# Cross attention keys: three of four groups turned by DVE in 32 by 32 blocks and transfers through DRAM, in place of PE transposes

## The chip, the core and the metric

The kernel runs on one core of a Trainium2 chip. The metric is the device time of one execution in microseconds (us). The engines are PE (TensorE: matmuls and transposes through an identity), DVE (VectorE), ACT (ScalarE), POOL (GpSimd) and SP (SyncE, which here only waits and issues DMAs). They run their own instruction streams and meet only at semaphores.

## The reference, cut to what matters

A decoder layer on 16 batches of 100 tokens of width 512: self attention, cross attention over 361 context rows per batch, and a ternary feed-forward. The change is in the cross attention:

```python
q = x @ Wq.T                                   # 32 heads of 16
k = rmsnorm(heads(context @ Wk.T)); v = heads(context @ Wv.T)
scores = einsum('bhnd,bhmd->bhnm', rmsnorm(q), k) * 16 ** -0.5
out = einsum('bhnm,bhmd->bhnd', softmax(scores), v)
```

## The kernel before, in words

Self attention comes first (to about 545 us), cross attention second (to about 1033 us), the feed-forward last. Only the middle stage is touched.

The 16 x 361 context rows are cut into 46 chunks of 126 rows (`KC`), regardless of where a batch ends. Batch b projects two or three new chunks (two only for batches 7 and 14, which the code calls `short`); the chunk on a border is shared by two batches. A chunk's projected keys lie with the rows on the partitions and 512 columns (4 groups of 8 heads of 16). The scores need them the other way round: 128 columns of a group on the partitions. So for each of the four groups t, `turn_heads(b, t)` transposes the 126x128 blocks of the two or three chunks on PE into the PSUM tile `B[0]`, and `keys_back(b, t)` copies them on ACT into `kT` (a second copy puts the shared rows into the next batch's half of `kT`).

`turn(b)` is one round of the stage on each engine, with the order written by hand. On PE a turn runs the six score units `scores2(b, 1)` to `scores2(b, 5)` and then `scores2(b+1, 0)`; unit u covers two of the twelve (group, chunk) pairs, so unit 0 needs group 0 alone, and unit 1 is the first that needs group 1. Between them lie the projections of batch b+1 (`project2`, twelve matmuls each: 1 to 3 keys, 4 to 6 values), the products with the values (`attend2`), queries (`project_q`, `turn_queries`), and the transposes of finished outputs (`out_turn`). `turn_heads(b, 2)` and `turn_heads(b, 3)` stand in turn b, `turn_heads(b+1, 0)` and `turn_heads(b+1, 1)` in turn b. In three turns (2, 7 and 12) `project2(b+2, 1)` is pulled ahead into the end of the turn, where it waits for `ctx_lo` (DVE, L1221).

The keys of batch b+1 are made during turn b: ACT copies the projections into `raw` and squares them (`keep_raw`), DVE sums and takes the inverse root (`square_sums`, `rms_start`, `rms_step`, the last of them L1282), POOL multiplies (`normed`, L595: one instruction for queries when there are new ones, then one for each chunk). DVE then goes on to `x2_lo`, `add_cross(.., 0)` (which waits for PE's `out_turn(.., 0)`), `queries_back` (L1298) and `ctx_lo`. PE's `turn_heads(b+1, 0)` waits for `queries_back`, as both use `B[0]`.

SP issues, in each turn b, `sixteenth(2b, 0)`, `sixteenth(2b+1, 1)` (L520, parts of the feed-forward weights, first eight turns) and `context(b+2)` (L513), each behind waits.

Of the kernel before, what the change touches and what calls it, by code (L numbers as in the profile page):

```python
# [6 lines left out]
F32 = mybir.dt.float32  # L7
# [19 lines left out]
KC = 126  # L27
NC = 3
# [185 lines left out]
def build(nc, x, wqkv, wo, wx, ctxt, wffn, gains, bcols, consts, rope, out):  # L214
    with ExitStack() as ctx:
# [45 lines left out]
        raw = [carve([KC, 4, 512]) for _ in range(2)]  # L261
# [7 lines left out]
        carve([128, 12288 - 4096 - 2 * CTXP * KT - 2 * NT * CTXP - 3 * XH * VW])  # L269
# [3 lines left out]
        e = carve([KC, 6, HT * S])  # L273

# [99 lines left out]

        A = [ctx.enter_context(nc.psum_tensor(f"A{i}", [128, 512], F32)) for i in range(2)]
# [4 lines left out]
        def hidden_banks(u, e):  # L380
# [24 lines left out]
                   pe_xT2=1, pe_q=1, pe_qT=1, pe_proj=6, pe_T=4, pe_sc=6, pe_pv=4, pe_oT=2,  # L405
                   a_ctx=1, a_x2=1, a_sqq=1, a_sq2=3, a_v2=3, a_T=4, a_e=6, a_o=4, a_abs=3,
                   d_xn2=1, d_ctx=1, d_x2=1, d_ssqq=1, d_ssq2=3, d_rstd2=1, d_qT=1, d_on=2, d_x2out=2,
                   g_qn=1, g_kn=3, g_m=1,
# [26 lines left out]
        g_ones = sem("g_ones")  # L435
        d_warm, a_ws, g_wlo, a_z = sem("d_warm"), sem("a_ws"), sem("g_wlo"), sem("a_z")
# [28 lines left out]
        def _(sp):  # L465
# [59 lines left out]

            context(0)
            context(1)
            sp.wait_ge(*count("d_x1", TL - 1, 1))
            for b in range(NB - 2):
                if b < NB // 2:  # L530
                    sixteenth(2 * b, 0)
                    sixteenth(2 * b + 1, 1)
                context(b + 2)
                if b == NB // 2:
                    for n in range(2):
                        sp.wait_ge(*count("a_abs", NB - 2 + n, 3))
                        tile(n)
                elif b == NB // 2 + 3:
                    sp.wait_ge(d_tern, 2)
                    tile(2)  # L540

            for n in range(3, 12):
# [6 lines left out]
                tile(n)  # L549

# [8 lines left out]
        def _(pool):  # L559
# [95 lines left out]
            pool.memset(kT[:, :, :, 2 * KC:CTXP], 0.0)  # L655
# [32 lines left out]
        def _(act):  # L688
# [115 lines left out]
            def keep_raw(b, n, par):  # L804
# [4 lines left out]
                if n == 1:  # L809
                    act.wait_ge(*count("pe_T", b - 2, 4))  # L810
# [26 lines left out]
            def keys_back(b, t):  # L837

                act.wait_ge(*count("pe_T", b, t + 1))
# [3 lines left out]
                ins = act.activation(kT[:, b % 2, t, 0:whole], B[0][:, 0:whole], ACT.Copy)  # L843
                if b < NB - 1:
                    act.wait_ge(*count("pe_sc", b - 1, T_UNITS[t]))
                    ins = act.activation(kT[:, 1 - b % 2, t, 2 * KC + own:CTXP], B[0][:, tail + own:tail + KC], ACT.Copy)
                ins.then_inc(sig["a_T"], 1)

# [116 lines left out]
            keys_back(0, 0)  # L965
            keys_back(0, 1)
# [5 lines left out]
            def turn(b, par, end):  # L972
# [5 lines left out]
                keys_back(b, 2)  # L978
# [7 lines left out]
                keys_back(b, 3)  # L986
# [25 lines left out]
                if end < 2:  # L1012
                    if not short(b + 1):
                        values(b + 1, 2, odd)
                    keys_back(b + 1, 0)
# [8 lines left out]
                if end < 2:  # L1024
                    keys_back(b + 1, 1)
# [50 lines left out]
        def _(dve):  # L1076
# [211 lines left out]
            def queries_back(i):  # L1288
# [12 lines left out]
                ins.then_inc(sig["d_qT"], 1)  # L1301

# [284 lines left out]
            add_attn(TL - 1, A[0])  # L1587
            x2_lo(1, B[0])
            square_sums_q(1)

            def turn(b, par, end):
# [25 lines left out]
                else:  # L1617
# [6 lines left out]
                    ternary(4, 0)  # L1624
                if end == 1:
# [3 lines left out]
                if x2_tile(b) is not None:  # L1629
                    x2_lo(x2_tile(b), B[0])  # L1630
                if o2_tile(b) is not None:
                    add_cross(o2_tile(b), 0)
                if end == 1:
# [96 lines left out]
        def _(pe):  # L1730
# [143 lines left out]
            def turn_heads(b, t, par):  # L1874
# [4 lines left out]
                ins.then_inc(sig["pe_T"], 1)  # L1879

            def scores2(b, u):
                if u == 0:
                    pe.wait_ge(*count("a_T", b, 1))
                    pe.wait_ge(*count("d_qT", last_tile(b), 1))
                if u > 0:
# [3 lines left out]
                for f in range(2):  # L1889
                    t, c = divmod(2 * u + f, NC)  # L1890
                    for r in range(RT):
                        ins = pe.matmul(C[r][0:KC, f * 2 * S:(f + 1) * 2 * S],  # L1892
                                        kT[32 * r:32 * r + 32, b % 2, t, c * KC:(c + 1) * KC],
# [414 lines left out]
```

## Time and profile before

| what | value |
|---|---|
| three runs | 1312.74, 1312.95 and 1315.94 us, median 1312.95 |
| the profiled execution | 1312.68 us; its span, first to last instruction, 1310.9 us |
| PE busy | 1268.3 us, 97% of the span |
| DVE, ACT, POOL busy | 781.7, 648.9 and 295.8 us |
| PE transposes of the keys (L1878) | 184, 32.4 us busy |
| DMA engines' share over the span | 13.4% on the queue of the program's own transfers |

Sums are made against the profiled execution. An instruction's busy time overlaps its neighbours' on PE, so what a group costs is read from start to start in the timeline, not from its busy time.

### The profile page before, as it was taken

To read this page: it belongs to the slowest core of one execution; us is meant where nothing else is said; L and a number is where in the kernel's file an instruction comes from. 1 tells how busy PE (TensorE), PEld (TensorE's weight loads), DVE (VectorE), ACT (ScalarE), POOL (GpSimd) and SP (SyncE) were. 2 spreads that over 40 slices of the span, in tenths; PEclk is the share of its full clock that TensorE was granted. 3 is DMA by queue.
4 is the path that set the end of the run, shared out by engine and by line. 5 is a ranking of instruction groups with operands and counts; after the bars stand their busy time and mean duration, and the time that the engine had idled before them with its cause. 6 is when DMAs were issued, how large, how long until landed. Compare 5 with 4: busy or idle time off the path is not lost.

```text
span 1310.9 us, 27154 instructions
## 1 busy us (share of the span) xinstructions
PE 1268.3 (97%) x10784; PEld 850.2 (65%) x10784; DVE 781.7 (60%) x1890; ACT 648.9 (50%) x1524; POOL 295.8 (23%) x293
## 2 busy tenths in 40 slices
PE   8989999999999999999999999999999999999998
PEld 7656666666666666566666666666666665666554
DVE  6897788777877787434344434554455784443423
ACT  4663344343433356377777776666665523232221
POOL 0564454334334451111101101111101121000000
PEclk9999999999999999999999999999999999999999
DMA  8102000000000021112222222001012310000000
GB/s 330 73 9 73 9 8 10 7 3 9 9 8 9 9 88 63 72 32 84 105 73 73 74 73 89 25 25 58 25 58 84 125 52 24 1 24 1 24 1 30
DMA packets 18744, 63.98 MB, mean 49 GB/s; under 512 B 1850, under 2 KB 3386, under 8 KB 15418
## 3 DMA queue, kind: packets, MB, share of 16 engines
q1 hardware_dynamic: 18618, 62.24, 13.4%
q8 instruction: 86, 1.41, 0.4%
q14 instruction: 40, 0.33, 0.1%
HBM read 55.68 MB, written 3.28 MB: 45 GB/s over the span
## 4 chain that ended last, share of the span: by engine, by line
PE 83%; DVE 6%; issue 5%; ACT 4%; POOL 2%; DMA 0%; POOLq 0%; SPq 0%; DVEq 0%; ACTq 0%
PE A L1861 18%; PE A L1761 11%; PE C L2214 10%; PE A L1824 10%; PE C L1892 6%; PE B L1912 4%; PE C L1789 3%; PE A L2233 3%; PE A L1842 3%; PE B L2233 2%; PE C L1806 2%; PE A L1770 2%; PE B L1781 2%; PE B L1878 1%; PE B L1797 1%
## 5 line engine op out<-in xcount | busy, mean ns | idle before, releaser
L1861 PE MATMUL A<-wxhl,arena 128*126 128x512 f16 x1104 | 254.7, 381 | 3.2 <-DVE arena L1221 2.6
L1861 PEld LDWEIGHTS A<-wxhl,arena 128*126 128x126 f16 x1104 | 145.4, 136 | 86.3 <-issue 8.1
L1761 PE MATMUL A<-arena,wxhl 128*125 128x512 f16 (+1 forms) x780 | 174.5, 380 | 1.3 <-DVE tub L1140 1.3
L855 ACT ACTIVATE arena<-C 126x1600 f32<-126x1600 f32 x96 | 144.4, 1504 | 22.3 <-PE C L1892 22.3
L595 POOL TENSOR_TENSOR arena<-arena,region 126x512 f32<-126x512 f32 (+2 forms) x59 | 60.9, 1062 | 405.8 <-DVE region L1282 405.8
L1761 PEld LDWEIGHTS A<-arena,wxhl 128*125 128x125 f16 (+1 forms) x780 | 103.5, 136 | 62.1 <-DVE tub L1140 5.3
L2214 PE MATMUL C<-arena 128*128 128x375 f16 (+1 forms) x768 | 138.8, 333 | 0.0
L758 ACT ACTIVATE region<-C,negm 100x100 f32<-100x100 f32 x256 | 84.3, 358 | 100.8 <-DVE negm L1183 100.8
L569 POOL TENSOR_TENSOR region<-tub 125x512 f32<-125x512 f32 (+1 forms) x65 | 82.5, 1269 | 219.3 <-DVE tub L1140 217.0
L1824 PE MATMUL A<-arena,stageb 128*125 128x512 f16 (+1 forms) x416 | 124.0, 379 | 2.1 <-ACT qk L829 1.3
L2214 PEld LDWEIGHTS C<-arena 128*128 128x128 bf16 x768 | 74.8, 97 | 58.8
L1043 ACT ACTIVATE arena<-C,fsc 128x375 f32<-128x375 f32 (+1 forms) x63 | 37.4, 594 | 142.8 <-PE C L2214 142.8
L1667 DVE SCALAR_TENSOR_TENSOR arena<-C,fsc,arena 128x375 f32<-128x375 f32 (+1 forms) x63 | 40.0, 634 | 112.2 <-ACT arena L1043 111.8
L1824 PE MATMUL A<-arena,alo 128*125 128x512 f16 (+1 forms) x208 | 78.8, 379 | 0.0
L1259 DVE TENSOR_REDUCE region<-region 126x32 f32<-126x512 f32 x46 | 31.4, 684 | 76.1 <-ACT region L816 76.1
L1912 PE MATMUL B<-arena 126*17 126x100 f32 (+2 forms) x2752 | 75.0, 250 | 0.0
L578 POOL TENSOR_TENSOR region<-region,rstd 125x512 f32<-125x512 f32 (+1 forms) x61 | 63.9, 1077 | 48.2 <-DVE rstd L1090 48.2
L1824 PEld LDWEIGHTS A<-arena,stageb 128*125 128x125 f16 (+1 forms) x416 | 54.5, 135 | 29.9 <-issue 1.9
L741 ACT ACTIVATE sq<-A 125x512 f32<-125x512 f32 (+1 forms) x65 | 38.9, 598 | 69.6 <-PE A L1761 69.6
L1221 DVE SCALAR_TENSOR_TENSOR arena<-arena 128x1512 f16<-128x1512 f32 x16 | 27.8, 1740 | 67.5 <-ACT arena L782 67.5
L1912 PEld LDWEIGHTS B<-arena 126*17 126x17 f32 (+2 forms) x2752 | 57.2, 97 | 14.3 <-issue 14.3
L585 POOL TENSOR_TENSOR region<-region,rinv 100x400 f32<-100x400 f32 x64 | 58.6, 921 | 21.5 <-DVE rinv L1189 21.0
(201 smaller groups left out, 2256.5 us busy)
## 6 DMA issues: line engine op xcount, KB each, us to landing
stageb<-in_wffn SPq DMA_DIRECT2D x16, 768.0 KB, 4.8
arena<-in_ctxt SPq DMA_DIRECT2D x16, 756.0 KB, 5.8
stageb<-in_wffn SPq DMA_DIRECT2D x8, 1024.0 KB, 6.2
arena<-in_wqkv SPq DMA_DIRECT2D x4, 1024.0 KB, 12.1
wxhl<-in_wffn SPq DMA_DIRECT2D x4, 1024.0 KB, 4.7
arena<-in_wx SPq DMA_DIRECT2D x3, 1024.0 KB, 8.4
out_x<-xres SPq DMA_DIRECT2D x12, 224.0 KB
xres<-in_wo SPq DMA_DIRECT2D x2, 1024.0 KB, 19.3
```

Source lines behind the costliest of these rows:

```text
L569: pool.tensor_tensor(zb[0:n, j], tb[0:n, j % 2], ub[0:n, j % 2], ALU.add).then_inc(sig["g_w"], 1)
L578: pool.tensor_tensor(z, z, r, ALU.mult).then_inc(sig["g_z"], more)
L595: pool.tensor_tensor(t, t, r, ALU.mult).then_inc(sig[done], 2 if slot == 1 and last == 1 else 1)
L758: act.activation(pr[:, n * S:(n + 1) * S], C[g][0:S, h * S:(h + 1) * S], ACT.Exp, bias=negm[:, n:n + 1], scale=-1.0, accum_out=rsum[:, n:n ...
L855: act.activation(e[:, at:at + 2].rearrange("p f (r s) -> p r f s", r=RT), Call[0:KC, :].rearrange("p (r x) -> p r x", r=RT)[:, :, 0:4 * S] ...
L1761: ins = pe.matmul(A[j % 2][0:m, :], xp[:, k, at:at + m], wp[:, j, k, :], start=(n == 0), stop=(n == 11))
L1824: ins = pe.matmul(bank[0:m, :], ap[:, h, at:at + m], wohl[:, g, part, h % 4, :], start=(n == 0), stop=(n == 47))
L1861: ins = pe.matmul(A[(par + n) % 2][0:KC, :], xp[:, k, c * KC:(c + 1) * KC], wp[:, 1 if n < 4 else 2, k, :], start=(i == 0), stop=(i == 11))
L1892: ins = pe.matmul(C[r][0:KC, f * 2 * S:(f + 1) * 2 * S], kT[32 * r:32 * r + 32, b % 2, t, c * KC:(c + 1) * KC], qms[b % 2][32 * r:32 * r + ...
L1912: ins = pe.matmul(B[1][32 * j:32 * j + VW, g * S:(g + 1) * S], v[0:rows, at:at + VW], e[0:rows, (t * NC + c) % 6, h * S:(h + 1) * S], star ...
L2214: ins = pe.matmul(hidden_banks(u, e)[half][:, 0:cols], wf[3 * (e // 4) + half][:, k, (e % 4) * 128:(e % 4 + 1) * 128], part[:, k, 0:cols], ...
L2233: ins = pe.matmul((A + B)[r][0:n, :], part[e % 2][:, r * TW:r * TW + n], wf[3 * (e // 4) + 2][:, e % 4, :], start=(e == 0 and part is hh), ...
```

## The change

Group 0 is left as it was (PE, then ACT, now into `kT0`), and so is batch 0 in all groups, on semaphores of its own. For batches 1 to 15 the groups 1 to 3 go another way:

1. DVE, `turn_keys(b, c)`: for each chunk c, one instruction transposes all 32 by 32 blocks of `raw[:, c, 128:512]` (128 partitions, 384 columns) into `kts[:, c]`.
2. SP, `keys_out(b, c)`: four DMAs for each chunk (one for each 32 partitions), 48 KB each, put the blocks into their places in a DRAM buffer, in 384 runs of 128 bytes.
3. SP, `keys_in(b)`: when the four writes of chunk 0 and the four of chunk 1 have landed, one DMA (384 KB) brings both chunks of all three groups back into `kTd`; a second brings chunk 2. `keys_shared(b)` brings the shared rows for the next batch.
4. PE waits for these landings at `scores2(b, 1)` and `scores2(b, 2)`. The 129 transposes and ACT's copies of groups 1 to 3 of batches 1 to 15 are gone.

On SP all this stands in the one queue: in turn b, `keys_shared(b)` between the two `sixteenth`, and `keys_in(b+1)` behind `context(b+2)`. On DVE `turn_keys(b+1, 0)` and `(b+1, 1)` stand behind `x2_lo` and ahead of `row_stats3` and `add_cross(.., 0)`; `turn_keys(b+1, 2)` stands behind `add_cross(.., 0)` and ahead of `row_scales3` and `queries_back`.

```diff
-        kT = carve([128, 2, NT, CTXP])
+        kT0 = carve([128, 2, CTXP])
+        kTd = carve([128, 2, NT - 1, NC * KP])
+        kts = carve([128, NC, KW])
+        kd01 = nc.dram_tensor("keys01", (2, 128, NT - 1, 2, KP), F32).ap()
+        kd2 = nc.dram_tensor("keys2", (2, 128, NT - 1, KP), F32).ap()
...
+            def keys_out(b, c):
+                sp.wait_ge(*count("d_kt", b, c + 1))
+                for n in range(4):
+                    block = slice(32 * n, 32 * n + 32)
+                    if c < 2:
+                        dst = kd01[b % 2].rearrange("(r j) t c n -> c j t r n", r=4)[c][:, :, :, block]
+                    else:
+                        dst = kd2[b % 2].rearrange("(r j) t n -> j t r n", r=4)[:, :, :, block]
+                    sp.dma_start(dst, kts[block, c].rearrange("j (t r i) -> j t r i", t=NT - 1, r=4)).then_inc(kw[c], 16)
+            def keys_in(b):
+                for c in range(2 if short(b) else NC):
+                    keys_out(b, c)
+                sp.wait_ge(*written(0, b))
+                sp.wait_ge(*written(1, b))
+                sp.wait_ge(*count("pe_sc", b - 2, NU))
+                sp.dma_start(kTd[:, b % 2, :, 0:2 * KP], kd01[b % 2].rearrange("p t c n -> p t (c n)")).then_inc(kr01, 16)
+                if not short(b):
+                    sp.wait_ge(*written(2, b))
+                    own = own_rows(b)
+                    sp.dma_start(kTd[:, b % 2, :, 2 * KP:2 * KP + own], kd2[b % 2][:, :, 0:own]).then_inc(kr2, 16)
+            def keys_shared(b):
+                sp.wait_ge(*count("pe_sc", b - 1, NU))
+                own = own_rows(b)
+                src = kd01[b % 2][:, :, 1] if short(b) else kd2[b % 2]
+                sp.dma_start(kTd[:, 1 - b % 2, :, 2 * KP + own:2 * KP + KC], src[:, :, own:KC]).then_inc(krx, 16)
...
                 if b < NB // 2:
                     sixteenth(2 * b, 0)
+                if b > 0:
+                    keys_shared(b)
+                if b < NB // 2:
                     sixteenth(2 * b + 1, 1)
                 context(b + 2)
+                keys_in(b + 1)
...
+            keys_shared(NB - 2)
             for n in range(3, 12):
...
+                if n == 3:
+                    keys_in(NB - 1)
...
+            def turn_keys(b, c, par):
+                dve.wait_ge(*count("g_kn", b, c + 1))
+                dve.wait_ge(*written(c, b - 1))
+                dve.transpose(kts[:, c], raw[par][:, c, 128:512])\
+                   .then_inc(sig["d_kt"], 2 if c == 1 and short(b) else 1)
...
+                if x2_tile(b) is not None:
+                    x2_lo(x2_tile(b), B[0])
+                if end < 2:
+                    turn_keys(b + 1, 0, odd)
+                    turn_keys(b + 1, 1, odd)
                 if end == 1:
                     row_stats3(0, range(len(unit_tiles(0))))
                 if o2_tile(b) is not None:
                     add_cross(o2_tile(b), 0)
+                if end < 2 and not short(b + 1):
+                    turn_keys(b + 1, 2, odd)
...
             def scores2(b, u):
+                elif b > 0 and u == 1:
+                    pe.wait_ge(kr01, 16 * b)
+                elif b > 0 and u == 2:
+                    pe.wait_ge(*own_landed(b))
+                    pe.wait_ge(krx, 16 * (b - 1))
...
-                turn_heads(b, 2, par)
+                if b == 0:
+                    turn_heads(0, 2, 0)
...
-                pe.wait_ge(*count("a_T", b, 3))
-                turn_heads(b, 3, par)
+                if b == 0:
+                    turn_heads(0, 3, 0)
...
-                if end < 2:
-                    turn_heads(b + 1, 1, odd)
```

## Rows read from the trace of the kernel before

**Rows 1.** The page: busy time of the engines, and the granted clock.

```profile
PE 1268.3 (97%) x10784; PEld 850.2 (65%) x10784; DVE 781.7 (60%) x1890; ACT 648.9 (50%) x1524; POOL 295.8 (23%) x293
...
PEclk9999999999999999999999999999999999999999
```

**Rows 2.** The chain that ended last, by line, 560 to 1030 us.

```profile
by line: PE A L1861 47.0%; PE C L1892 16.9%; PE B L1912 10.8%; PE A L1842 6.1%; PE B L1878 3.7%; PE B L1920 2.3%; ACT arena L829 1.7%; issue 1.6%; ACT arena L855 1.4%; PE B L1871 1.4%; PE B L1833 1.3%; DVE arena L1221 1.1%; ACT qk L829 0.9%
```

**Rows 3.** PE in order of time, turn 5: start, length, line, shapes.

```profile
711.59 0.96 PE L1892 MATMUL C<-region,arena 32*126 32x200 f32 x16
...
715.12 0.49 PE L1878 MATMUL B<-cst,arena 126*128 126x126 f32 x3
715.45 2.75 PE L1861 MATMUL A<-wxhl,arena 128*126 128x512 f16 x12
...
739.91 0.54 PE L1878 MATMUL B<-cst,arena 126*128 126x126 f32 x3
740.29 2.75 PE L1842 MATMUL A<-wxhl,tub 128*125 128x512 f16 x12
742.97 0.96 PE L1892 MATMUL C<-qk,arena 32*126 32x200 f32 x16
```

**Rows 4.** PE in order of time: a short batch's group, and the start of turn 14.

```profile
774.80 0.38 PE L1878 MATMUL B<-cst,arena 126*128 126x126 f32 x2
775.02 2.75 PE L1861 MATMUL A<-wxhl,arena 128*126 128x512 f16 x12
...
986.17 0.96 PE L1892 MATMUL C<-qk,arena 32*126 32x200 f32 x16
```

**Rows 5.** PE in order of time: the projection pulled ahead in turn 2, idle in brackets.

```profile
646.95 2.80 PE L1861 MATMUL A<-wxhl,arena 128*126 128x512 f16 x12 [0.85 <-DVE arena L1221]
```

**Rows 6.** ACT's copies of the turned keys: min/median/max ns of one.

```profile
L843 ACT ACTIVATE arena<-B x64: 358/438/507, 547.0 to 1022.2; 128x252 f32<-128x252 f32 x8, 128x361 f32<-128x361 f32 x4, 128x344 f32<-128x344 f32 x4, 128x327 f32<-128x327 f32 x4
```

**Rows 7.** POOL in order of time: the multiplications of turns 4, 5 and 13.

```profile
696.76 4.10 POOL L595 TENSOR_TENSOR arena<-arena,region 125x512 f32<-125x512 f32 x4 [28.60 <-DVE region L1282]
...
729.36 4.11 POOL L595 TENSOR_TENSOR arena<-arena,region 125x512 f32<-125x512 f32 x4 [28.31 <-DVE region L1282]
...
976.29 2.07 POOL L595 TENSOR_TENSOR arena<-arena,region 126x512 f32<-126x512 f32 x2 [25.24 <-DVE region L1282]
```

**Rows 8.** Groups by line and shape: DVE over 375 columns, busy us, mean ns.

```profile
L1679 DVE TENSOR_TENSOR arena<-arena 128x375 f16<-128x375 f32 x32 | 17.6, 550 | 10.7 <-ACT arena L1055 10.4
```

**Rows 9.** SP's issues of `sixteenth` and of whole tiles, min/median/max ns.

```profile
L520 SPq DMA_DIRECT2D stageb<-in_wffn x16: 539/545/664, 547.3 to 773.3; - x16
L524 SPq DMA_DIRECT2D stageb<-in_wffn x8: 327/328/424, 801.2 to 1053.1; - x8
```

**Rows 10.** SP in order of time: two of them in a row.

```profile
547.35 1.32 SPq L520 DMA_DIRECT2D stageb<-in_wffn  x2
```

**Rows 11.** The page's DMA issues: count, KB each, us from issue to landing.

```profile
stageb<-in_wffn SPq DMA_DIRECT2D x16, 768.0 KB, 4.8
...
xres<-in_x SPq DMA_DIRECT2D x1, 256.0 KB, 2.9
```

**Rows 12.** SP's waits: the one for the last store, total, times, longest.

```profile
SPq L215 <- DMA out_x<-xres: 2.2, 1, 2.2
```

**Rows 13.** DMA packets, MB, share of 16 engines: 733-740, 831-839, 1305-1311 us.

```profile
q1 hardware_dynamic: 400, 0.79, 35.7%
...
q1 hardware_dynamic: 144, 0.77, 29.5%
...
q1 hardware_dynamic: 582, 0.97, 52.2%
```

**Rows 14.** DVE in order of time, end of turn 14.

```profile
1003.22 1.87 DVE L1333 BATCH_NORM_STATS2 stats<-xres 125x6 f32<-125x512 f32 x3
...
1010.48 0.99 DVE L1298 TENSOR_TENSOR region<-B,cst 128x800 f32<-128x800 f32 x1
```

**Rows 15.** PE in order of time, end of turn 14 and start of turn 15.

```profile
1011.53 0.54 PE L1878 MATMUL B<-cst,arena 126*128 126x126 f32 x3 [1.04 <-DVE region L1298]
...
1016.97 0.96 PE L1892 MATMUL C<-region,arena 32*126 32x200 f32 x16
```

More of the change, by code:

```diff
@@ L27 @@
 KC = 126
+KP = 128
+KW = 3 * 128
 NC = 3
@@ L260, in build @@
         carve = carver()
-        raw = [carve([KC, 4, 512]) for _ in range(2)]
+        raw = [carve([128, 4, 512]) for _ in range(2)]
         ctxs = carve([128, KT, CTXP])
@@ L435, in build, with written, own_landed @@
         g_ones = sem("g_ones")
+        pe_T0, a_T0 = sem("pe_T0"), sem("a_T0")
+        kw = [sem(f"kw{c}") for c in range(NC)]
+        kr01, kr2, krx = sem("kr01"), sem("kr2"), sem("krx")
+        def written(c, b):
+            return kw[c], 4 * 16 * sum(c < 2 or not short(n) for n in range(1, b + 1))
+        def own_landed(b):
+            return kr2, 16 * sum(not short(n) for n in range(1, b + 1))
         d_warm, a_ws, g_wlo, a_z = sem("d_warm"), sem("a_ws"), sem("g_wlo"), sem("a_z")
@@ L1884, in scores2 @@
                     pe.wait_ge(*count("d_qT", last_tile(b), 1))
+                elif b == 0 and u != 2 and u < 5:
+                    pe.wait_ge(a_T0, {1: 1, 3: 2, 4: 3}[u])
+                elif b > 0 and u == 1:
+                    pe.wait_ge(kr01, 16 * b)
+                elif b > 0 and u == 2:
+                    pe.wait_ge(*own_landed(b))
+                    if b == 1:
+                        pe.wait_ge(a_T0, 3)
+                    else:
+                        pe.wait_ge(krx, 16 * (b - 1))
                 if u > 0:
@@ L1891, in scores2 @@
                     for r in range(RT):
-                        ins = pe.matmul(C[r][0:KC, f * 2 * S:(f + 1) * 2 * S],
-                                        kT[32 * r:32 * r + 32, b % 2, t, c * KC:(c + 1) * KC],
-                                        qms[b % 2][32 * r:32 * r + 32, t].rearrange("p f s -> p (f s)"), start=True, stop=True)
+                        group = slice(32 * r, 32 * r + 32)
+                        keys = kTd[group, b % 2, t - 1, c * KP:c * KP + KC] if t else kT0[group, b % 2, c * KC:(c + 1) * KC]
+                        ins = pe.matmul(C[r][0:KC, f * 2 * S:(f + 1) * 2 * S], keys,
+                                        qms[b % 2][group, t].rearrange("p f s -> p (f s)"), start=True, stop=True)
                 ins.then_inc(sig["pe_sc"], 1)
@@ L2112, in _ @@
             turn_heads(0, 1, 0)
-            pe.wait_ge(*count("a_T", 0, 2))
+            pe.wait_ge(a_T0, 1)
             x2_turn(1, B[0])
@@ L2197, in turn @@
                 if end < 2:
-                    pe.wait_ge(*count("a_T", b + 1, 2))
+                    pe.wait_ge(*count("a_T", b + 1, 1))
                 if o2_tile(b) is not None:
```

58 lines of the change are left out of this document (34 added, 24 removed).

## The prediction

> **What bounds the kernel now.** I read the page first: PE is busy for 97% of the span, the next engine for 60%, and the granted clock is full in every slice [rows 1]. Then the chain of work that ended last, inside the cross attention: it hardly leaves PE, and the key transposes (L1878) are 3.7% of those 470 us, 17 us for all four groups [rows 2]. So the stage is bound by what PE is given, and a PE instruction taken out is worth its place in PE's queue, as long as nothing else becomes late. The timeline of a turn then gives the places: a turn is 31.4 us, from one `scores2(b, 1)` at 711.59 to the next at 742.97 [rows 3].
>
> **What it removes.** From start to start a group of three transposes takes 0.33 us behind a projection (715.12 to 715.45) and 0.38 us behind a product with the values (739.91 to 740.29) [rows 3]; a group of two takes 0.22 us [rows 4], and 0.27 us in the two other places of the short batches. For batches 1 to 14:
> - group 2: nine full batches at 0.33, three at 0.38 (turns where the projection was pulled ahead), two short ones at 0.22: 4.6 us;
> - group 3: twelve at 0.38, two at 0.27: 5.1 us;
> - group 1: twelve at 0.38, but in turns 2, 7 and 12 PE waits for DVE's `ctx_lo` right behind it, 0.85 us of idle [rows 5], and `ctx_lo` does not come sooner, so there the gain is nothing: nine at 0.38 and two at 0.27, 4.0 us.
>
> Sum 13.6 us. ACT loses 45 long copies of 0.44 us [rows 6] and as many short ones, but PE hardly waits for ACT; I count nothing for it. `turn_heads(b, 0)` stays, with the wait on its copy.
>
> **What it adds, on the way of the keys.** This is new latency, hidden if it ends before PE comes to `scores2(b+1, 1)`. It starts at POOL: four instructions take 4.1 us [rows 7], 1.03 each, the first one for queries, so chunk 0 is ready 2.06 us after POOL's start (1.03 without queries). DVE's block transpose is not in the trace; the nearest row, 375 f32 columns, took 0.55 us [rows 8]. Below it could not take less than nothing; above, 1.1 us if each column passed twice. I take 0.55, with 0.05 for the handover.
>
> The Trainium skill, VectorE: DVE Perf Modes, "The three transpose paths", gives 311 ns for a 128 by 128 bf16 tile turned in such blocks (and advises TensorE where PSUM will do as the target); three tiles would be an estimated 0.93 us instead of 0.55, and by it the sum would lose about 1.5 us, in the four turns without slack. No run here shows it yet.
>
> Then SP. Each chunk is four DMAs of 384 runs of 128 bytes. The trace has one kind with 384 runs, `sixteenth`: one issue took 0.54 to 0.66 us [rows 9], and two in a row 1.32 us [rows 10], so 0.66 a piece. The bounds are 0.33 below, the median issue of a whole tile, one run for each partition [rows 9], and above, the DMA engines themselves. Their price per packet: the 384 packets of 2 KB of one load took 35.7% of 16 engines for 7 us, 104 ns each; the 128 of 6 KB, 29.5% for 8 us, 295 ns each; the 475 stores of 2 KB at the end 52.2% for 6 us, 105 ns each [rows 13]. A line through the two loads gives 6 ns and 0.048 ns a byte: 12 ns for 128 bytes. A short store to DRAM is not in the trace: floor 12 ns, ceiling 105 ns. Each engine gets 24 packets of a DMA, 0.29 us at the floor, 2.5 us at the ceiling. I take the floor's neighbourhood, anything up to 27 ns, since load and store of 2 KB cost the same here; then SP's 0.66 sets the pace, and twelve issues take 7.8 us.
>
> The Trainium skill, DMA: Bandwidth & Descriptors, "Specifications", says that transfers under 512 bytes are read, modified and written, which speaks against this change. Were each short store worth two passes, it would be an estimated 24 ns and still under 27: the sum is the same, with next to no margin. No row here shows it.
>
> The read back of 384 KB is issued behind all twelve writes. 768 KB landed 4.8 us after issue and 256 KB 2.9 us after [rows 11]; between them, 3.3 us. The writes of chunks 0 and 1 have landed by then (2.2 us for a last store [rows 12], and four more issues lie between). So from chunk 0 turned to keys in place: 7.8 + 3.3 = 11.1 us. A short batch has eight writes and must wait for the last: 5.2 + 2.2 + 3.3 = 10.7 us.
>
> **The room for it.** Turn 5: POOL starts at 729.36 [rows 7], chunk 0 is turned at 732.0; PE comes to `scores2(6, 1)` at 742.97 [rows 3], less the 0.38 of the group removed between: 10.6 us. Turns 0 and 10 have 10.9. Turn 4: turned at 699.4, needed at 711.59 [rows 3] less 0.38: 11.8 us; so have turns 1, 9 and 11. Turns 2, 3, 7, 8, 12 have 12.4 to 12.8, and turn 6, a short batch, 12.5. Turn 13 is a short batch in a turn with little else: POOL starts at 976.29 [rows 7], turned at 977.9, needed at 986.17 [rows 4] less 0.27: 8.0 us. PE stalls where the room is short, and such a stall moves everything behind it: 0.2 in turns 0 and 10, 0.5 in turn 5, 2.7 in turn 13: 3.6 us. Chunk 2 (its own read, needed by `scores2(b, 2)` two projections later, over 5 us) is hidden by those projections; without that cover it would cost 3 us a turn.
>
> **Who waits behind the new waits.** DVE stands at `turn_keys` for POOL, but `add_cross(.., 0)`, next in its queue, starts for PE's `out_turn` within 0.1 us of that time in the turns with queries: nothing. The third `turn_keys` moves `queries_back` by 0.6 us; PE's `turn_heads(b+1, 0)` has about 1 us of slack there, by the projection between, and short batches have no third. On SP `context(b+2)` stands ahead of the wait; the next `sixteenth` goes out some 8 us later and is needed some 15 us after that. In turn 14 the same order costs: DVE did `row_stats3` (1.87 us) while POOL worked [rows 14], and now does it after two waits and two transposes, a third transpose follows, and `queries_back` comes at 1013.5 instead of 1010.48 [rows 14]. PE already waited 1.04 us for it [rows 15], so all 3 us reach `turn_heads(15, 0)`. `scores2(15, 1)` at 1016.97 [rows 15] had 1.1 us in group 1 and its copy's wait that now vanish, and the exponentials of 1.5 us set the pace behind: 1.9 later there, 0.3 won back when groups 2 and 3 go. 1.6 us lost.
>
> **The sum.** 13.6 - 3.6 - 1.6 = 8.4 us gained: 1312.7 (profiled execution) becomes 1304.3; the median of the runs is 0.3 above it, so 1304.5.
>
> **The rivals.** Everything hangs on x, what the way of the keys takes beyond 11.1 us. Turns 0, 5, 10 and 13 lose x at once, turns 1, 4, 9 and 11 lose x - 0.7, the other six x - 1.6.
> - *The DMA engines pace the writes, and it is slower.* At 35 ns a packet (midway between 12 and 105 by ratio) a write takes 0.84 us, twelve take 10.1, x = 2.3: 9.2 + 6.4 + 4.2 = 19.8 us lost, 1324. At 40 ns x = 3.7 and 1344; at the ceiling of 105 ns x = 22, some 295 us lost, 1600. It decides from x = 1.8, a write of 0.81 us (34 ns). For it: 4,600 packets a batch against 18,618 in the whole program before, and slack of under 1 us in most turns. Against: the floor from the two loads.
> - *No change.* x from 0.9 to 1.8, by pitch, by reads queued behind the writes, or by the transpose: 1309 to 1316, about 1312.
> - *All of it arrives in time.* If SP issues in 0.35 us, the way takes 7.5 us, and 8.3 in the short turn, 0.3 too long: only the 1.6 of turn 14 is lost, 1301.
>
> **How the numbers follow.** A difference under 0.3% (3.9 us) cannot be told from none on this kernel. My forecast 0.33, in time 0.13, no change 0.16, slower 0.38. Faster is the first two, 0.46. The single likeliest case has its own range of 1300 to 1309. The range for eight in ten: down to 1298 (no stall, nothing lost in turn 14, and 1 us for ACT), up to 1345, the DMA-paced case at 40 ns; above it I leave about 0.15, below 0.03.
>
> **What would show it.** PE in order of time: an idle entry at `scores2(b, 1)` put down to a DMA into `arena`, near 0 in most turns and near 2.7 us in turn 13. SP's timeline: runs of writes at 0.66 a piece; 0.8 or more proves me wrong, and so does a write whose DMA share stays high after SP is done. DVE: 43 transposes near 0.55 us. POOL's idle and start in each turn should move only with PE. Turn 14: `queries_back` about 3 us after where it stood. Wrong would make it: short stores slower than 27 ns, an issue of this shape dearer than `sixteenth`, or a read back that lands later than 3.3 us.

## The result, and the profile after

| | before | changed |
|---|---|---|
| median of six runs each | 1313.95 us (1312.57 to 1315.94) | 1319.77 us (1318.78 to 1321.13) |
| ratio, 95% interval | | 1.0044 (1.0031 to 1.0056) |
| profiled execution, and its span | 1312.68 and 1310.9 us | 1320.37 and 1318.5 us |
| PE busy | 1268.3 us | 1260.1 us |
| DVE, ACT, POOL busy | 781.7, 648.9, 295.8 us | 803.8, 631.0, 295.5 us |

Slower by 0.44%, where the forecast was 0.6% faster. The page of the changed kernel (busy time, granted clock, packets, the queue of the program's transfers, and two kinds of issue with KB and us to landing):

```profile
PE 1260.1 (96%) x10655; PEld 840.8 (64%) x10655; DVE 803.8 (61%) x1933; ACT 631.0 (48%) x1437; POOL 295.5 (22%) x294
...
PEclk9999999999999999999999999999998999999999
...
DMA packets 104344, 80.84 MB, mean 61 GB/s; under 512 B 81690, under 2 KB 88986, under 8 KB 101018
...
q1 hardware_dynamic: 104218, 79.11, 19.5%
...
keys<-arena SPq DMA_DIRECT2D x172, 48.0 KB, 2.1
...
arena<-keys SPq DMA_DIRECT2D x15, 384.0 KB, 4.1
```

The work did leave PE (8 us less busy), and the packets multiplied by 5.6 while the queue's share of the engines rose only from 13.4% to 19.5%. New is a digit of 8 in the row of the clock, near 1000 us, where the row before has 9 throughout [rows 1]. Then PE in order of time (the figure in brackets is how long PE stood idle just before, and what ended it); L1985 is `scores2`, L1952 `turn_queries`:

```profile
554.37 0.96 PE L1985 MATMUL C<-qk,arena 32*126 32x200 f32 x16
...
588.30 1.47 PE L1985 MATMUL C<-region,arena 32*126 32x200 f32 x16 [2.80 <-issue]
...
596.15 0.96 PE L1985 MATMUL C<-region,arena 32*126 32x200 f32 x16
...
714.62 0.96 PE L1985 MATMUL C<-region,arena 32*126 32x200 f32 x16 [0.66 <-DMA arena<-keys]
...
1015.26 0.93 PE L1952 MATMUL B<-cst,arena 100*128 100x100 f32 x4 [2.11 <-DVE region L1454]
...
1035.52 0.96 PE L1985 MATMUL C<-region,arena 32*126 32x200 f32 x16 [1.05 <-ACT arena L923]
```

The same two places in the kernel before (L1892 is its `scores2`):

```profile
553.56 0.96 PE L1892 MATMUL C<-qk,arena 32*126 32x200 f32 x16
...
1027.69 0.96 PE L1892 MATMUL C<-region,arena 32*126 32x200 f32 x16 [1.05 <-ACT arena L855]
```

The stage, from `scores2(0, 1)` at 554.37 to `scores2(15, 5)` at 1035.52, takes 481.15 us; before it was 553.56 to 1027.69, 474.13 us. So 7.0 of the 7.6 us by which the span grew lie here, 0.8 ahead of the stage, where nothing was edited, and -0.2 behind it. The eight idle entries at `scores2(b, 1)`, at the ends of turns 0, 1, 4, 5, 9, 10, 11 and 13, are 2.80, 0.35, 0.66, 0.99, 0.52, 1.87, 0.22 and 2.49 us: 9.9 us. Three of them (turns 0, 5 and 10) are labelled "issue" and are the same wait: in turn 0 the read that PE needs was issued at 583.16 and landed 5.05 us later, 0.09 us before PE went on; in turns 5 and 10 it is 0.09 us too. SP in order of time (L554 the writes, L563 the read back of chunks 0 and 1), in turns 0, 5, 10 and 13:

```profile
574.50 8.54 SPq L554 DMA_DIRECT2D keys<-arena  x12
583.16 1.91 SPq L563 DMA_DIRECT2D arena<-keys  x1
...
734.10 7.91 SPq L554 DMA_DIRECT2D keys<-arena  x12
742.12 1.09 SPq L563 DMA_DIRECT2D arena<-keys  x1
...
886.71 8.69 SPq L554 DMA_DIRECT2D keys<-arena  x12
895.51 0.56 SPq L563 DMA_DIRECT2D arena<-keys  x1
...
979.74 5.25 SPq L554 DMA_DIRECT2D keys<-arena  x8
987.13 0.56 SPq L563 DMA_DIRECT2D arena<-keys  x1
```

Two of the forecast's numbers stand in these rows. Twelve writes in 7.91 us are 0.66 a piece. And PE comes when it was said to; the room is the time from chunk 0 turned until PE comes for it. In turn 5 chunk 0 is turned at 734.08 and PE is there at 746.07 less 0.99, a room of 11.0 us where 10.6 was forecast; turn 4 has 11.9 for 11.8, turn 0 11.0 for 10.9, turn 10 11.0 for 10.9, turn 13 8.5 for 8.0. Only turn 6 is far off, 11.3 for 12.5, and its keys came just in time. What is longer is the way of the keys (from chunk 0 turned until PE has them), forecast at 11.1 us: 12.0 in turn 5, 12.5 in turn 4, 12.9 in turn 10, 13.8 in turn 0; in turn 13 11.0 where 10.7 was forecast. All rows of that read (min, median, max):

```profile
L563 SPq DMA_DIRECT2D arena<-keys x15: 560/561/1906, 583.2 to 1020.1; - x15
...
DMA to landing us min/median/max: 3.5/4.1/5.1
```

It landed 4.1 us after issue, not 3.3. The writes' packets are cheap. A window of 9 us with twelve writes in it (packets, MB, share of 16 engines):

```profile
q1 hardware_dynamic: 4400, 0.54, 35.2%
```

That is 16 x 9 x 0.352 = 50.7 us for 4400 packets, 11.5 ns each, for 128 bytes. The forecast took 12; the ceiling of 105 and the rival's 35 are far off. (The Trainium skill, DMA: Bandwidth & Descriptors, "Specifications", has transfers under 512 bytes read, modified and written; in the packet times of these writes to DRAM no second pass is to be seen.) DVE's side, as one line of the source and then in order of time at the end of turn 14:

```profile
L1375 DVE STREAM_TRANSPOSE arena<-arena x43: 570/578/581, 573.9 to 1015.6; 128x384 f32<-128x384 f32 x43
...
  POOL arena L652: 31.5, 33
```

```profile
1012.76 1.84 DVE L1408 BATCH_NORM_STATS2 stats<-xres 125x6 f32<-125x512 f32 x3
1014.51 0.24 DVE L1453 RECIPROCAL region<-B 125x16 f32<-125x16 f32 x1
...
1018.84 0.99 DVE L1366 TENSOR_TENSOR region<-B,cst 128x800 f32<-128x800 f32 x1
```

A transpose took 0.578 us (forecast 0.55; by the estimate from the Trainium skill, VectorE: DVE Perf Modes, "The three transpose paths", it would have been 0.93, so the measurement goes with the row). But DVE stands 31.5 us at them for POOL, and `add_cross(.., 0)` stands behind: in turn 14 it came at 1014.51, PE's `turn_queries` waited 2.11 us for it, and `queries_back` came at 1018.84, 28.1 us after the turn's start at 990.72, where it had come at 1010.48, 24.3 us after 986.17 [rows 14, rows 4]: 3.8 us later in the turn, where 3 was forecast. Of these 1.6 are the lower clock at the turn's start, below.

Last, the granted clock. Windows of 4 us: busy time of PE, PEld, DVE, ACT and POOL with instructions, then PE's granted clock, the DMA engines' share and GB/s:

```profile
588.30:592.30 4.00, 4.00 (x23) 2.47 (x24) 0.00 (x0) 1.50 (x1) 0.00 (x0) 0.57 1.02 310
...
899.50:903.50 4.00, 3.92 (x30) 2.63 (x31) 0.05 (x1) 1.70 (x2) 0.00 (x0) 1.00 0.70 225
...
990.70:994.70 4.00, 3.98 (x23) 2.31 (x24) 0.02 (x1) 1.50 (x1) 0.00 (x0) 0.58 0.63 246
...
1015.20:1019.20 4.00, 3.94 (x13) 2.58 (x14) 3.52 (x20) 0.00 (x0) 0.00 (x0) 0.57 0.43 74
```

After the idles of 2.80 (turn 0), 2.49 (turn 13) and 2.11 us (turn 14) PE ran for most of 4 us at the lower level, 1.2 GHz; after 1.87 us in turn 10 it did not. From `scores2(1, 1)` to `scores2(1, 2)` it took 7.85 us in place of 6.21 (as in fillers_early below), and from `scores2(14, 1)` to `scores2(14, 2)` the same: 1.64 us each that no idle entry shows. The third stretch at the lower level, behind 2.11 us, cost nothing: it fell where PE would otherwise have stood 1.47 us for `queries_back` (pe_unhindered below), and turn 14 takes 32.66 us both in fillers_early, where the clock falls there, and in fillers, where it does not.

### The profile page after: what moved, and what is told of

Its sections match the earlier page's. It is cut to its first block and busy times, and to the rows that moved or that the text cites. A ratio compares the mean times of both kernels' runs of the same rounds, so it can differ in the third digit from the quotient of the medians.

```text
span 1318.5 us, 27126 instructions
## 1 busy us (share of the span) xinstructions
PE 1260.1 (96%) x10655; PEld 840.8 (64%) x10655; DVE 803.8 (61%) x1933; ACT 631.0 (48%) x1437; POOL 295.5 (22%) x294
## 2 busy tenths in 40 slices
DMA packets 104344, 80.84 MB, mean 61 GB/s; under 512 B 81690, under 2 KB 88986, under 8 KB 101018
## 3 DMA queue, kind: packets, MB, share of 16 engines
q1 hardware_dynamic: 104218, 79.11, 19.5%
## 5 line engine op out<-in xcount | busy, mean ns | idle before, releaser
L1942 PE MATMUL A<-wxhl,arena 128*126 128x512 f16 x1104 | 257.5, 386 | 4.6 <-DVE arena L1289 4.0
```

What stands on the lines that cost most here:

```text
L1942: ins = pe.matmul(A[(par + n) % 2][0:KC, :], xp[:, k, c * KC:(c + 1) * KC], wp[:, 1 if n < 4 else 2, k, :], start=(i == 0), stop=(i == 11))
```

## The experiments

All ratios are to the kernel before on the same chip. A book by turns goes through them: the length of a turn, from one `scores2(b, 1)` to the next, worked out from these starts in each trace, in us. Not shown are turns 7 and 12, which go much as turn 2; turns 3, 6 and 8, where the kernels with the change agree within 0.1 us; and turns 4, 9 and 11, where pe_part wins 1.0 us as in turn 1 and the changed kernel is 0.7, 1.2 and 0.3 us behind it (pe_unhindered 0.6 in turn 9). "last" is the stretch from 1016.97 to 1027.69 of before.

```
turn      before  pe_part  pe_unhindered  changed  reordered_three_dims
0         31.40   31.07    31.07          33.93    31.06
1         32.27   31.28    31.28          33.34    31.28
2         32.89   32.24    32.65          32.65    32.23
5         31.38   30.39    30.39          31.45    30.38
10        31.39   30.40    30.40          32.35    30.40
13        24.14   23.57    24.40          26.94    23.57
14        30.80   30.06    32.67          34.31    30.97
last      10.72   10.40    10.40          10.49    10.49
stage    474.13  461.94   467.25         481.15   462.98
```

**pe_part.** What is the PE side worth alone?

```diff
-                if end < 2:
-                    turn_keys(b + 1, 0, odd)
-                    turn_keys(b + 1, 1, odd)
...
-                keys_in(b + 1)
...
-                    pe.wait_ge(kr01, 16 * b)
...
-                        keys = kTd[group, b % 2, t - 1, c * KP:c * KP + KC] if t else kT0[group, b % 2, c * KC:(c + 1) * KC]
+                        keys = kTd[group, 0, t - 1, c * KP:c * KP + KC] if t else kT0[group, b % 2, c * KC:(c + 1) * KC]
```

> Leaves out: the block transposes on DVE, all transfers of keys to and from DRAM, and the waits on them; PE uses the first batch's keys for the heads of groups 1 to 3 in every batch. What stays is the PE side of the change alone: 45 groups of transposes and their copies gone. My theory (the 13.6 us of PE time are a real gain, and all of it is eaten by what stands in their place): 1312.7 - 13.6, less about 0.5 for waits on ACT's exponentials in the two short turns, about 1299.5 to 1300.5, ratio 0.990. Rival one (the turns were paced by the copies and exponentials on ACT too, so taking PE work out gives back little): 1306 to 1311, and the idle of PE in the cross attention grows by the difference.

Measured: 1300.1 us, ratio 0.9906 (0.9892 to 0.9919). PE in order of time, start and end of the stage:

```profile
552.93 0.96 PE L1965 MATMUL C<-qk,arena 32*126 32x200 f32 x16
...
1014.87 0.96 PE L1965 MATMUL C<-region,arena 32*126 32x200 f32 x16 [1.05 <-ACT arena L916]
```

461.94 us, 12.2 less than before. The gain is real, and rival one is out. It is less than was forecast, though: the 13.6 us stood for batches 1 to 14 alone, and their part is 11.1 us in turns 0 to 13 and 0.4 in turn 14, 11.6 in all. A plain turn wins 0.99 us (forecast 0.33 + 0.38 + 0.38 = 1.09): a group behind a product with the values frees 0.33 us, not the 0.38 that stand from start to start. Turns 6 and 13 win 0.55 and 0.57 where 0.98 was forecast, for in each PE now stands 0.53 us at `scores2(b, 3)` for ACT's exponentials, a wait that the kernel before does not show.

**pe_unhindered.** Everything runs, PE waits for none of the transfers (SP gets some waits of its own, so that the reads stay apart; they are not shown).

```diff
-                sp.dma_start(kTd[:, b % 2, :, 0:2 * KP], kd01[b % 2].rearrange("p t c n -> p t (c n)")).then_inc(kr01, 16)
+                sp.dma_start(kTd[:, 1, :, 0:2 * KP], kd01[b % 2].rearrange("p t c n -> p t (c n)")).then_inc(kr01, 16)
...
-                    pe.wait_ge(kr01, 16 * b)
...
-                        keys = kTd[group, b % 2, t - 1, c * KP:c * KP + KC] if t else kT0[group, b % 2, c * KC:(c + 1) * KC]
+                        keys = kTd[group, 0, t - 1, c * KP:c * KP + KC] if t else kT0[group, b % 2, c * KC:(c + 1) * KC]
```

> Everything that the change adds runs as in the changed kernel (block transposes, writes, reads back), but PE waits for none of it: it uses the first batch's keys for groups 1 to 3, and all reads land in a half of the key buffer that PE does not read after the first batch. My theory: PE loses only what DVE brings later: some 1.6 us in four turns at turn_queries, and in turn 14 about 3.5 us with its clock drop, so 1303.5 to 1306; the difference to the changed kernel (14 to 16 us) is the price of late keys. Rival two (the 80 MB of small packets and DVE's reads and writes of SBUF slow down matmuls or other engines by contention): no faster than 1310, with longer single instructions. A third (the waits on DVE are most of the loss): over 1312.

Measured: 1305.85 us, 0.9945 (0.9933 to 0.9958). PE, at `turn_queries` in turns 9 and 14, and at `turn_heads(15, 0)`:

```profile
849.00 0.65 PE L1963 MATMUL B<-cst,arena 125*128 125x125 f32 x4 [0.56 <-DVE region L1465]
...
1000.75 0.56 PE L1963 MATMUL B<-cst,arena 100*128 100x100 f32 x4 [2.12 <-DVE region L1465]
...
1005.37 0.54 PE L1970 MATMUL B<-cst,arena 126*128 126x126 f32 x3 [1.47 <-DVE region L1377]
```

The window behind the 2.12 us (columns as above), at the full clock:

```profile
1001.00:1005.00 4.00, 2.90 (x16) 1.64 (x14) 3.55 (x19) 0.60 (x1) 0.00 (x0) 1.00 0.43 74
```

The stage is 5.3 us longer than in pe_part, and the book says where: 2.6 in turn 14, 0.8 in turn 13, and 1.9 in turns 2, 7, 9 and 12 together. All other turns are equal to 0.02 us, with 81,690 short packets in one kernel and 1,850 in the other. So no contention shows, and all of it lies where PE waits for `add_cross` or `queries_back`: 0.34 to 0.56 us at `turn_queries` in turns 2, 7, 9 and 12, 1.27 at `turn_heads` in turn 13, and the rows above in turn 14. The changed kernel is 13.9 us longer still: that is the price of late keys, with what the lower clock adds behind the waits for them.

**write_pairs.** Is SP's price one of the instruction or of the run?

```diff
                 for n in range(4):
                     block = slice(32 * n, 32 * n + 32)
-                    if c < 2:
-                        dst = kd01[b % 2].rearrange("(r j) t c n -> c j t r n", r=4)[c][:, :, :, block]
...
+                    if c == 1:
+                        dst = kd01[b % 2].rearrange("m j (c n i) -> n j c m i", n=4, i=32)[n]
+                        src = kts[block, 0:2].rearrange("j c (m i) -> j c m i", i=32)
+                    else:
+                        dst = kd2[b % 2].rearrange("m j (n i) -> n j m i", n=4)[n]
+                        src = kts[block, 2].rearrange("j (m i) -> j m i", i=32)
+                    sp.dma_start(dst, src).then_inc(kw[c // 2], 16)
```

> Chunks 0 and 1 are written together, by four DMAs of 768 runs of 128 bytes in place of eight of 384 (the layout in DRAM is turned so that the read back is still one DMA); they start when chunk 1 is turned, 1.03 us later. If SP's price is one of the instruction (0.66 us): eight issues take 5.3 us in place of 7.9, the way of the keys is 1.6 us shorter, nearly all waits for keys outside turn 13 vanish: 1309 to 1312. Rival (the price goes by the run: 128 runs took 0.33 us, 384 took 0.66, so 768 take about 1.2): four writes take 4.8 us, the way is as long as before or up to 1 us longer: 1319 to 1328.

Measured: 1309.58 us, 0.9972 (0.9963 to 0.9981). SP in order of time: the first two and the last two of the eight writes of turn 5:

```profile
730.34 0.63 SPq L556 DMA_DIRECT2D keys<-arena  x1
...
731.01 0.65 SPq L556 DMA_DIRECT2D keys<-arena  x1
...
734.30 0.47 SPq L556 DMA_DIRECT2D keys<-arena  x1
...
734.81 0.47 SPq L556 DMA_DIRECT2D keys<-arena  x1
```

A write of 768 runs goes out 0.67 to 0.70 us behind the one before, one of 384 runs 0.66 in the changed kernel: the price is the instruction's and not that of its runs. One write of 1536 runs for a whole chunk was planned too and never ran. Waits for keys are left in turn 0 (1.20 us) and 13 (1.95). Unasked for, the writes of chunk 2, which have three dimensions here in place of four, go out 0.51 us apart.

**chunk0_alone.** `scores2(b, 1)` reads group 1's chunk 0 and nothing of chunk 1.

```diff
-                for c in range(2 if short(b) else NC):
-                    keys_out(b, c)
+                keys_out(b, 0)
+                keys_out(b, 1)
                 sp.wait_ge(*written(0, b))
+                sp.wait_ge(*count("pe_sc", b - 2, NU))
+                sp.dma_start(kTd[:, b % 2, :, 0:KP], kd01[b % 2][:, :, 0]).then_inc(kr0, 16)
+                if not short(b):
+                    keys_out(b, 2)
                 sp.wait_ge(*written(1, b))
-                sp.wait_ge(*count("pe_sc", b - 2, NU))
-                sp.dma_start(kTd[:, b % 2, :, 0:2 * KP], kd01[b % 2].rearrange("p t c n -> p t (c n)")).then_inc(kr01, 16)
+                sp.dma_start(kTd[:, b % 2, :, KP:2 * KP], kd01[b % 2][:, :, 1]).then_inc(kr1, 16)
```

> One part alone: the read back of chunks 0 and 1 is cut in two, and chunk 0, all that scores2(b, 1) needs, is read as soon as SP has issued the writes of chunk 1; chunk 2's writes stand behind it. My theory (PE's stalls are for a read that stands behind twelve issues of 0.66 us): the read of chunk 0 is issued 5.3 us after its first write, not 7.9 to 8.5, and lands some 9 us after it: waits for keys only in turn 13 (under 2 us) and perhaps turn 0, clock 1.00 everywhere except perhaps turn 14: 1306 to 1310. Rival (the reads are late because of traffic or of a slow read back behind the small packets, whatever the order): the landing grows in place of the queue, 1315 or more.

Measured: 1307.35 us, 0.9959 (0.9946 to 0.9972). One wait for keys is left:

```profile
978.85 0.96 PE L1989 MATMUL C<-qk,arena 32*126 32x200 f32 x16 [0.80 <-DMA arena<-keys]
```

The stage is 468.15 us, 0.9 longer than pe_unhindered: with the read ahead of four issues, 13 of the 13.9 us of late keys are gone. The traffic is the same, so it was not the traffic. Two things changed together: the read goes out sooner (in turn 5 5.36 us after the first write in place of 8.02), and, being half as large, it lands sooner (median 3.0 us in place of 4.1). The place in SP's queue is the larger part; no run takes the two apart.

**stats_first.** The part of turn 14 that the forecast priced at 1.6 us.

```diff
+                if end == 1:
+                    dve.wait_ge(*count("d_x2out", unit_tiles(0)[-1], 2))
+                    row_stats3(0, range(len(unit_tiles(0))))
                 if end < 2:
                     turn_keys(b + 1, 0, odd)
                     turn_keys(b + 1, 1, odd)
-                if end == 1:
-                    dve.wait_ge(*count("d_x2out", unit_tiles(0)[-1], 2))
-                    row_stats3(0, range(len(unit_tiles(0))))
```

> One part alone: in turn 14 DVE's row_stats3 stands ahead of its two turn_keys again, so that it runs while POOL works. My theory: add_cross, and with it turn_queries and queries_back, come 1.8 us sooner, the idle ahead of turn_queries falls from 2.1 to about 0.3 us and the clock stays at 1.00 behind it (another 1.4 us): 1316.5 to 1318.5 against 1319.8 of the changed kernel. Rival (the keys of batch 15 land when they land, and PE only waits for them in place of DVE): 1319 to 1320, with a new wait for the DMA at scores2(15, 1).

Measured: 1320.46 us, 1.0054 (1.0038 to 1.0070), as the changed kernel. PE:

```profile
1013.78 0.56 PE L1952 MATMUL B<-cst,arena 100*128 100x100 f32 x4 [0.34 <-DVE region L1454]
...
1025.09 1.46 PE L1985 MATMUL C<-region,arena 32*126 32x200 f32 x16 [1.49 <-DMA arena<-keys]
...
1028.25 1.71 PE L1985 MATMUL C<-region,arena 32*126 32x200 f32 x16 [0.68 <-ACT arena L923]
```

The rival is right. `turn_queries` waits 0.34 us in place of 2.11, but the keys of batch 15 land when they land, `scores2(15, 1)` waits 1.49 us for them, and the clock falls there instead (0.58 and then 0.50 over the next 4 us). In turn 14 two delays lay side by side; taking one away shows the other.

**fillers and fillers_early.** Is the clock's drop a cost of its own? The second hunk is in fillers alone.

```diff
                 elif b > 0 and u == 1:
+                    if b in (1, 14):
+                        pe.wait_ge(*count("a_e", b, u))
+                        for _ in range(10):
+                            pe.matmul(C[0][:, 0:128], ident, ident, start=True, stop=True)
                     pe.wait_ge(kr01, 16 * b)
...
+                if end == 1:
+                    pe.wait_ge(*count("a_v2", b + 1, 1))
+                    for _ in range(8):
+                        pe.matmul(A[(odd + 6) % 2][:, 0:128], ident, ident, start=True, stop=True)
```

> The changed kernel with idle time of PE filled: ten matmuls of 128 by 128 (0.23 us each) ahead of the wait for the read back in batches 1 and 14, and eight ahead of the wait for DVE's add_cross in turn 14. They do no useful work and write banks that are written over next. My theory (after these three idles the granted clock was at 0.57 for some 3 to 4 us, costing 1.65, 1.7 and 1.4 us): clock 1.00 in all three windows, about 1315 to 1316, 3.5 to 4.8 us faster than the changed kernel. Rival (the clock drop is not set off by the idle, but by something else there, or it just moves to the next wait): 1319 to 1320, windows still at 0.57.

> The changed kernel with ten matmuls of 0.12 us a pass ahead of the wait for the read back in batches 1 and 14 alone; the fillers of turn 14 are left out. If the clock's drop behind these two idles is a cost of its own: 1.65 + 1.7 = 3.3 us less than the changed kernel, 1316 to 1317. If it is paid back later whatever one does (as the total of the first run with fillers, 1320.2, could mean): 1319 to 1320.5.

Measured: fillers 1320.2 us, 1.0057 (1.0044 to 1.0071); fillers_early 1319.45, 1.0040 (1.0025 to 1.0056). Windows of fillers_early, then PE in order of time:

```profile
587.90:591.90 4.00, 4.00 (x31) 2.64 (x32) 0.00 (x0) 1.78 (x2) 0.00 (x0) 1.00 1.01 301
988.10:992.10 4.00, 3.99 (x31) 2.64 (x32) 0.00 (x0) 1.77 (x2) 0.00 (x0) 1.00 0.59 227
```

```profile
587.90 0.96 PE L1989 MATMUL C<-region,arena 32*126 32x200 f32 x16 [0.59 <-DMA arena<-keys]
...
594.11 0.96 PE L1989 MATMUL C<-region,arena 32*126 32x200 f32 x16
...
1029.49 0.52 PE L2008 MATMUL B<-arena 126*17 126x100 f32 x11 [1.50 <-issue]
```

In the windows the theory holds: the clock stays at 1.00 and the stretch behind takes 6.21 us in place of 7.85. In the total it was not confirmed: the medians are those of the changed kernel. The traces show where the gain goes: turns 1 and 14 together are 3.2 and 3.3 us shorter than in the changed kernel, and the last stretch takes 13.12 us in fillers and 12.34 in fillers_early in place of 10.49. In that stretch both traces (spans 1316.4 and 1316.3, against 1318.5) have an idle entry, of 2.30 and 1.50 us, in the middle of `attend2(15, 1)` that none of the others has and that waits for nothing that the profile shows. So about 3.3 us is the clock's price where it was read, but that it can be had back this way is not shown.

**changed_again.** 

> The changed kernel once more, unedited, beside the next two on the same chip: 1319 to 1321, as before. A rival reading of the first result (chance of that chip) would want less than 1316.

Measured: 1319.99 us (1315.46 to 1323.51), 1.0039 (1.0021 to 1.0058). Its profiled execution, one of 1323.51, has the same idles and more of the lower clock: after turn 0's wait of 2.66 us the stretch takes 9.27 us in place of 6.21, and there is now a drop behind turn 10's wait, as long as the 1.87 us that had none:

```profile
900.75 0.96 PE L1985 MATMUL C<-region,arena 32*126 32x200 f32 x16 [1.85 <-issue]
901.64 7.08 PE L1942 MATMUL A<-wxhl,arena 128*126 128x512 f16 x24
908.65 0.62 PE L1985 MATMUL C<-region,arena 32*126 32x200 f32 x8
```

7.90 us in place of 6.21. Thirteen runs of the changed kernel spread over 8.1 us, the five of the next kernel over 3.0, and the twelve of the kernel before, beside this run, over 4.4: part of the change's cost seems to differ from one execution to the next. Not all of that is the change's, for this trace also has the lower clock twice in the first 90 us, where nothing was edited.

**reordered.** Both single parts (chunk0_alone and stats_first) and two more edits: POOL takes chunk 0 ahead of the queries, and DVE's `add_cross` stands between the first and the second `turn_keys`.

```diff
-                for rows, slot, done in q + [(KC, c, "g_kn") for c in range(last + 1)]:
+                k = [(KC, c, "g_kn") for c in range(last + 1)]
+                for rows, slot, done in k[:1] + q + k[1:] if b > 0 else q + k:
...
                 if o2_tile(b) is not None:
                     add_cross(o2_tile(b), 0)
+                if end < 2:
+                    turn_keys(b + 1, 1, odd)
```

> Both parts above, and two more: POOL normalizes chunk 0 ahead of the queries (the way of the keys starts 1.03 us sooner in turns with queries), and DVE's add_cross(.., 0) stands between the first and the second turn_keys, so that PE's turn_queries does not wait for POOL. My theory: no wait for keys but under 1.5 us in turn 13, none at turn_queries; left of the loss is what DVE and the transfers cost beyond that, so near pe_unhindered or better: 1303 to 1306, faster than before by 0.5 to 0.7%. Rival (transfers slow the rest down wherever they stand): 1309 or more.

Measured: 1303.79 us (1303.55 to 1306.53), 0.9937 (0.9925 to 0.9949). The forecast held: the waits at `turn_queries` are gone, one wait for keys of 1.21 us is left in turn 13.

**reordered_three_dims.** That kernel, with the layout of write_pairs but a write for each chunk and block.

```diff
-                        dst = kd01[b % 2].rearrange("(r j) t c n -> c j t r n", r=4)[c][:, :, :, block]
-                    sp.dma_start(dst, kts[block, c].rearrange("j (t r i) -> j t r i", t=NT - 1, r=4)).then_inc(kw[c], 16)
+                    kd = kd01[b % 2][:, :, c] if c < 2 else kd2[b % 2]
+                    dst = kd.rearrange("m j (n i) -> n j m i", n=4)[n]
+                    sp.dma_start(dst, kts[block, c].rearrange("j (m i) -> j m i", i=32)).then_inc(kw[c], 16)
```

> As reordered, and the layout in DRAM is turned so that each write has three dimensions in place of four (same runs of 128 bytes, same number of DMAs). In write_pairs such writes went out 0.52 us apart in place of 0.66: by that the read of chunk 0 is issued 1.1 us sooner, the wait of 1.21 us in turn 13 all but vanishes: 1302 to 1303.5. If three dimensions do not help here: 1303.8 as before.

Measured: 1301.73 us (1300.75 to 1302.65), 0.9904 (0.9889 to 0.9919): 1% faster than before, and the best here. SP in turn 5, and PE at `scores2(14, 1)`:

```profile
727.28 3.91 SPq L552 DMA_DIRECT2D keys<-arena  x8
731.29 0.42 SPq L560 DMA_DIRECT2D arena<-keys  x1
```

```profile
976.27 0.96 PE L1989 MATMUL C<-qk,arena 32*126 32x200 f32 x16
```

Eight writes in 3.91 us are (3.91 - 0.47) / 7 = 0.49 us apart, and PE waits for no key at all. The stage is 1.0 us from pe_part, 0.9 of it in turn 14, where PE waits 1.95 us for `queries_back` in place of 1.04. So with every transpose and transfer of the change still running, nearly all of its loss is gone.

## Why the prediction was wrong

By its own terms, in us of the stage; a minus is time won:

| term | forecast | measured | where read |
|---|---|---|---|
| transposes of batches 1 to 14 leave PE | -13.6 | -11.6 | pe_part against before, without what belongs to batch 15 |
| PE waits for keys | +3.6 | +10.6 | changed against pe_unhindered, less the clock |
| DVE's order in turn 14, less what batch 15 wins | +1.6 | +2.0 | `turn_heads(15, 0)` 2.6 later than in pe_part, less 0.3 and 0.3 |
| DVE's order, other turns | 0 | +2.7 | pe_unhindered against pe_part |
| lower clock | 0 | +3.3 | turns 1 and 14, twice 1.64 |
| sum | -8.4 | +7.0 | |

- **The step that failed first is the way of the keys.** "11.1 us" was 12.0 to 13.8 in the turns where PE waited, but for turn 13. Its pitch, the 0.66 us from one write to the next, was right, and so were the rooms but for turn 6. Its landing was too short (4.1 for 3.3: interpolated from loads with longer runs and an emptier queue, when this read goes out right behind twelve writes; which of the two matters was not tested). From the first write's start to the read it was 8.0 us and not 7.8 even at best, and in turns 0 and 10 the twelve writes took 8.5 and 8.7; why is open. The seven turns 0, 1, 4, 5, 9, 10 and 11 had 0.7 us to spare or none at all, so an error of 0.9 to 2.7 us in 11 made 7.4 us of idle time of the 0.9 forecast for them; turn 13 waited 2.5 us, as forecast (2.7). The idle entries are 9.9 us in all; the other 0.7 of the 10.6 us is some 0.07 at each wait that no entry shows. The text had said of this, as "no change", x from 0.9 to 1.8 and some 1312: its x came true in most of these turns, its time did not, for the other terms stood beside it.
- **The gain was 2.0 us too high.** 0.38 us for a group behind a product with the values was 0.33, and "PE hardly waits for ACT; I count nothing for it" left out 0.53 us in turn 6 and again in turn 13 (pe_part).
- **"Nothing" for what stands behind DVE's wait was wrong.** `add_cross` was said to start for PE's `out_turn` within 0.1 us of DVE's wait for POOL; in five turns besides turn 14 it comes late enough, behind two waits and two transposes of 0.58 us, for PE to wait for it: 2.7 us. With `add_cross` ahead of the second `turn_keys` (reordered) these waits are gone.
- **Turn 14** was seen and nearly right, 2.0 for 1.6: `turn_heads(15, 0)` came 2.6 us late and not 3, but of the 1.1 us that were to vanish behind it only 0.3 did. What was not seen is that the keys of batch 15 are late there as well (stats_first).
- **The clock was left out.** The forecast priced a stall at its own length. Here the waits of 2.80 and 2.49 us for keys took another 1.64 us each with them. That these idles lower the clock is shown by the windows and by the fillers' windows; but it is no rule, for behind 2.12 us in pe_unhindered the clock stayed full. Why two equal idles differ stays open.
- **The transfers themselves were right**: 11.5 ns a packet for 12, no sign of the engines as the bound, no contention. The rival with 38 in 100, that the engines pace the writes, is false, though it is the one on whose side the time fell. The result lies inside the range by luck: the upper part of the range was drawn for that rival.

So the expected gain did not go missing. Over the whole stage, batch 15 included, 12.2 us came (pe_part) and 19.2 went: 5.3 to DVE's order and 13.9, with the clock's 3.3, to late keys, 13 of it gone once the read no longer stood behind four issues it did not need (chunk0_alone).

## What to carry to other kernels

When work leaves the bounding engine for a way over a queue, the way's length against the room decides, and it must be added up with every issue that stands ahead of the one result that is needed first; find that result (here one of three chunks) and let it go alone. Put new waits on an engine behind what others are waiting for, and reckon with a stall of 2 us or more on PE costing more than its length: here two of them cost another 1.64 us each, and some of over 2 us nothing. If a kernel's change loses, run it once without its waits: here that run and the changed one differed by 14 us, and reordering with one new layout turned 0.4% slower into 1% faster.

## What the runs showed of the hardware that was not expected

- SP's issue price hardly went by the runs: these writes in four dimensions went out 0.66 us apart with 384 runs and 0.67 to 0.70 with 768; in three dimensions, with another layout in DRAM, 0.49 to 0.51 with 384 runs. The rows of before had only suggested that more runs cost more [rows 9]. The number of dimensions alone does not set it either: `sixteenth`, also 384 runs and three dimensions, took 0.55 us (median) to issue in reordered_three_dims, where a write took 0.47.
- Packets of 128 bytes from SBUF to DRAM took 11.5 ns of an engine each.
- After idles of 1.95 (write_pairs), 2.11, 2.49 and 2.80 us (the changed kernel) the granted clock stood at 0.57 or 0.58 over the next 4 us; after 0.99 and 1.21 us at 1.00. In turn 10 it was 0.66 after 1.85 us, and 1.00 after 1.87 us and, in stats_first, after 2.03 us. In turn 14, where 2.11 us brought it down in the changed kernel, it stayed at 1.00 after 2.12 us in pe_unhindered, 2.11 in write_pairs and 2.10 in chunk0_alone; and in stats_first it fell after 1.49 us. So between 1.5 and 2.3 us both were seen, and the length of the idle alone does not decide it.
